# Second attention of a two-layer graph network: row sums from half-added P, and a new place for masks, low halves and statistics

## The reference, cut to what matters

```python
q, k, v = heads(features @ Wq), heads(features @ Wk), heads(features @ Wv)
e = jnp.einsum('whqd,whkd->whqk', q, k)
e = jnp.where(e >= 0, e, ALPHA * e)                      # ALPHA = 0.2
attn = jax.nn.softmax(jnp.where(adj[:, None] > 0, e, NEG), axis=-1)
h = jnp.einsum('whqk,whkd->whqd', attn, v)
out = _layernorm(h, g1, b1)
out = jnp.concatenate([out, features], axis=-1) @ Wffn.T
out = _layernorm(out, g2, b2)
return out + features
```

## Time and profile before

| | us |
|---|---|
| median of 3 runs | 3299.5 (3299.11 to 3303.42) |
| the profiled execution, its own time | 3305.43 |
| its span, first to last instruction | 3303.6 |
| mean granted TensorE clock | 0.98 |
| second attention, about | 1925 to 3303.6 |

### The profile page before, as it was taken

The page is one execution under the profiler, slowest core; times in us unless marked ns, Lnnn a source line. Parts: engine busy times, 40 slices in busy tenths (PEclk is TensorE's granted clock), DMA queues, the critical chain, the costliest instruction groups (busy, mean ns, idle before and its releaser), DMA issues. The chain is left out here.

```text
span 3303.6 us, 77256 instructions
## 1 busy us (share of the span) xinstructions
PE 3136.0 (95%) x29189; PEld 2106.8 (64%) x29189; DVE 2328.4 (70%) x6789; ACT 2009.7 (61%) x3727; POOL 1331.2 (40%) x1254
## 2 busy tenths in 40 slices
PE   7999999999999859999999959999999999999996
PEld 4666666666666536666666636777776677777674
DVE  5888888888888835655555536777777777777773
ACT  3666656666665535665555516676666666666674
POOL 2555555555555523443344321333333333333333
PEclk9999999999999979999999969999999999999998
DMA  5454444444444311111111123444444444444431
GB/s 154 134 145 131 137 140 138 133 137 145 131 135 143 107 58 39 52 50 42 52 52 52 39 83 116 132 134 132 135 134 131 129 130 130 133 138 130 129 124 45
DMA packets 290749, 365.80 MB, mean 111 GB/s; under 512 B 31680, under 2 KB 199232, under 8 KB 290368
## 3 DMA queue, kind: packets, MB, share of 16 engines
q1 hardware_dynamic: 289216, 359.25, 35.6%
q10 hardware_dynamic: 1152, 1.52, 0.2%
HBM read 242.16 MB, written 118.49 MB: 109 GB/s over the span
## 5 line engine op out<-in xcount | busy, mean ns | idle before, releaser
L1840 ACT ACTIVATE b_prob<-b_score_t 128x512 f32<-128x512 f32 x512 | 304.2, 594 | 367.3 <-PE b_score_t L2093 361.3
L2011 DVE CUSTOM_DVE_ANT_0 b_junk<-b_score,b_mask 128x256 bf16<-128x256 f32 x1024 | 390.6, 418 | 190.6 <-issue 183.8
L2428 DVE TENSOR_TENSOR f_gl<-f_act,f_gh 128x512 f16<-128x512 f32 x256 | 245.1, 958 | 285.1 <-ACT f_act L2350 285.1
L1909 POOL TENSOR_TENSOR b_nw_root<-b_nw_var,b_minus_halves 128x2 f32<-128x2 f32 x128 | 89.7, 701 | 841.4 <-DVE b_nw_neg_mean L1961 841.4
L1408 DVE TENSOR_TENSOR a_linked<-a_prob,a_mask 128x1024 f32<-128x1024 f32 x256 | 353.3, 1380 | 3.9 <-ACT a_prob L1205 3.9
L2345 ACT ACTIVATE f_gh<-f_up,s_f_b 128x512 f16<-128x512 f32 x256 | 175.5, 685 | 279.9 <-PE f_up L2476 279.9
L1205 ACT ACTIVATE a_prob<-a_score_t 128x1024 f32<-128x1024 f32 x256 | 259.3, 1013 | 109.6 <-PE a_score_t L1488 102.6
L1401 DVE TENSOR_REDUCE a_neg_max<-a_score 128x4 f32<-128x1024 f32 x256 | 307.0, 1199 | 4.1 <-PE a_score L1501 4.1
L1846 ACT ACTIVATE b_score_t<-b_score_t 128x512 f32<-128x512 f32 x512 | 303.5, 593 | 0.3 <-PE b_score_t L2102 0.3
L2474 PE MATMUL f_down<-s_w,f_gh 128*128 128x256 f16 x1024 | 279.1, 273 | 1.0 <-DVE f_gl L2428 1.0
L2476 PE MATMUL f_down<-s_w,f_gl 128*128 128x256 f16 x1024 | 279.1, 273 | 0.0
(11 more groups left out here) (234 smaller groups left out, 8990.7 us busy)
## 6 DMA issues: line engine op xcount, KB each, us to landing
a_stack<-qk_scratch SPq DMA_DIRECT2D x384, 128.0 KB, 3.0
b_stack<-qk_scratch SPq DMA_DIRECT2D x384, 128.0 KB, 2.8
qk_scratch<-a_qk SPq DMA_DIRECT2D x64, 512.0 KB, 2.9
qk_scratch<-b_qk SPq DMA_DIRECT2D x64, 512.0 KB, 2.8
a_x_sb<-x_t SPq DMA_DIRECT2D x64, 256.0 KB, 3.2
a_adj_sb<-adj_t SPq DMA_DIRECT2D x64, 256.0 KB, 3.2
a_res<-x_nodes SPq DMA_DIRECT2D x64, 256.0 KB, 3.4
after_attention<-a_z_out SPq DMA_DIRECT2D x64, 256.0 KB, 2.5
```

Source lines behind the costliest of these rows:

```text
L1840: nc.scalar.activation(prob[:, he], score_t[s][:].rearrange("p t n -> p (t n)"), ACT.Exp, scale=ALPHA).then_inc(exp_done, 1)
L2011: last = nc.vector.tensor_tensor_reduce(junk[:, s, it], score[s][:, it], mask[:, i, it], -1.0, 3e38, ALU.add, ALU.min, neg_max[:, i, col:c ...
L2428: nc.vector.tensor_tensor(gl[:, bu[1] % 2, f], act32[:, f % 2], gh[:, bu[1] % 2, f], ALU.subtract).then_inc(low_done, 1)
```

## The change

GpSimd gets four additions a graph (`halved`, steps 7, 1, 3 and 5): each adds the two key halves of P for two heads into `half_sum`, 128 x 512 f32. TensorE's sums no longer read P; they are two groups of four products on `half_sum`, `sums0` in step 5 and `sums1` in step 7, behind that step's value products. ScalarE's exp also waits for `half_done` before it overwrites P, and the copy of the sums (`evac_sums`) becomes an operation of its own in step 7. Six entries of `AT` move one step ahead: xh, q_hi, k_hi, v_out, linked and mask. On ScalarE z1, hh and z now stand before the copies of q, k, x and v. On VectorE the low halves stand first in their step and x's ahead of rinv, and statistics of the heads stand ahead of `zero_q`.

```diff
-    AT = {..., "xT": 8, "xh": 9, "xl": 9, "q": 10, "q_hi": 11, "q_lo": 11, "linked": 8, "k": 12, "k_hi": 13, "k_lo": 13,
-          ..., "v": 14, "v_out": 15, ..., "mask": 16, ..., "exp": 29, "values": 33, "res": 45,
-          "evac": 40, "turn_sum": 40, ...}
+    AT = {..., "xT": 8, "xh": 8, "xl": 9, "q": 10, "q_hi": 10, "q_lo": 11, "linked": 7, "k": 12, "k_hi": 12, "k_lo": 13,
+          ..., "v": 14, "v_out": 14, ..., "mask": 15, ..., "exp": 29, "halved": 31, "sums0": 37, "sums1": 39, "values": 33, "res": 45,
+          "evac": 40, "evac_sums": 39, "turn_sum": 40, ...}
+        half_sum = sb("half_sum", [P, H, N], F32)
@@ ScalarE, exp @@
                             act.wait_ge(values_done, n)
+                            act.wait_ge(half_done, n)
@@ ScalarE, copies @@
+                        nc.scalar.activation(heads_sb[:], heads_t[:], ACT.Copy).then_inc(heads_out, 1)
+                    if bv := due(t, h, "evac_sums"):
+                        act.wait_ge(sums_done, count(bv, 2, 2))
+                        if (n := after(back(bv, 1), 1, 1)) is not None:
                             act.wait_ge(sums_turned, n)
-                            act.wait_ge(heads_turned, n)
                         nc.scalar.activation(sums_sb[:], sums_t[:, 0:N], ACT.Copy).then_inc(sums_out, 1)
-                        nc.scalar.activation(heads_sb[:], heads_t[:], ACT.Copy).then_inc(heads_out, 1)
@@ GpSimd @@
+                    if half := half_due(t, h, "halved"):
+                        bv, k = half
+                        pool.wait_ge(exp_done, count(bv, H, 2 * k + 2))
+                        if k % 2 == 0 and (n := after(back(bv, 1), 2, k // 2 + 1)) is not None:
+                            pool.wait_ge(sums_done, n)
+                        pair = prob[:, 2 * k:2 * k + 2]
+                        nc.gpsimd.tensor_tensor(half_sum[:, 2 * k:2 * k + 2], pair[:, :, 0:N], pair[:, :, N:2 * N], ALU.add).then_inc(half_done, 1)
@@ TensorE @@
-                        for term in range(2):
-                            for a in range(HQ):
...
+                        for a in range(HQ):
+                            he = HQ * c + a
+                            last = nc.tensor.matmul(heads_t[DH * a:DH * (a + 1), c], values[...], prob[:, he, cols],
+                                                    start=jt == 0, stop=jt == 1)
+                        last.then_inc(values_done, 1)
+                    for c in range(DC):
+                        if bv := due(t, h, f"sums{c}"):
+                            pe.wait_ge(half_done, count(bv, HALVES, 2 * c + 2))
...
                             for a in range(HQ):
+                                last = nc.tensor.matmul(sums_t[DH * a:DH * (a + 1), 0:N], pick[:, c], half_sum[:, HQ * c + a], start=c == 0, stop=c == 1)
+                            last.then_inc(sums_done, 1)
```

More of the change, by code:

```diff
@@ L1894, in step @@
                         last.then_inc(z_ready, 1)
+                    for j, name in enumerate(("q", "k")):
+                        if bp := due(t, h, name + "_hi"):
+                            i = bp[1] % 2
+                            act.wait_ge(proj_done, count(bp, 4, j + 2))
+                            if j == 0 and exists(back(bp, 2)):
+                                act.wait_ge(qk_stored[i], uses(back(bp, 2), 2) * 16)
+                            nc.scalar.activation(qk[:, i, 2 * j], proj[:], ACT.Copy).then_inc(qk_high, 1)
+                    if bx := due(t, h, "xh"):
+                        act.wait_ge(proj_done, count(bx, 4, 1))
+                        if (n := after(back(bx, XB), 1, 1)) is not None:
+                            act.wait_ge(out_done, n)
+                        nc.scalar.activation(xh[:, bx[1]], proj[:],
+                                             ACT.Copy).then_inc(xh_ready, 1)
+                    if bp := due(t, h, "v_out"):
+                        act.wait_ge(proj_done, count(bp, 4, 4))
+                        if (n := after(back(bp, RING), HALVES, HALVES)) is not None:
+                            act.wait_ge(values_done, n)
+                        nc.scalar.activation(values[:, bp[1] % RING].rearrange("p t n -> p (t n)"), proj[:], ACT.Copy).then_inc(v_ready, 1)
             run_steps(act, step, STEPS_TAIL)
@@ L1975, in step @@
                                                 out_row[:].unsqueeze(1).to_broadcast([P, NT, D]), ALU.add).then_inc(y_ready, 1)
+                    if bx := due(t, h, "xl"):
+                        r = bx[1]
+                        dve.wait_ge(xh_ready, count(bx, 1, 1))
+                        nc.vector.tensor_tensor(xl[:, r], proj[:].rearrange("p (c n) -> p c n", c=DC), xh[:, r], ALU.subtract).then_inc(xl_ready, 1)
                     if bv := due(t, h, "rinv"):
```

60 lines of the change are left out of this document (18 added, 42 removed).

## The result

The changed kernel takes 3218.4 us (median of 4 runs, 3216.0 to 3219.5) where the kernel before takes 3299.3 (4 runs, 3297.7 to 3303.4): a ratio of 0.975, 95% interval 0.9735 to 0.9766, 81 us less. The forecast was 65 us less.

What follows compares the result with a forecast made beforehand. TensorE was taken to bound. Per graph -0.90 - 0.16 - 0.13 + 0.16 = -1.03 us, -59.7 over 58 graphs and -5.4 in six others, so 3299.5 - 65 = 3234.5 us; range 3209 to 3266.

Steps and rivals of the forecast that it cites:

- TensorE bounds, and a group is worth 0.45: TensorE, steps 1 and 3: no room in a graph; two removed groups of sums save 0.90 us a graph.
- The wait of v, -0.16: TensorE ahead of the products of v: the wait for k's low half goes, -0.16 us a graph.
- The DMA stall, -0.13: TensorE before the first score product: an earlier store shortens the DMA wait, -0.13 us a graph, between 0 and -0.18.
- The held-up root, +0.16: GpSimd's root of the heads' statistics, held by zeroing of q, delays TensorE's far product: +0.16 us, bounds 0 and 0.7.
- The slow end of the sum, 3251: Whole kernel: -0.90 + 0.16 = -0.74 us a graph, no wait won back, 48 us less.
- the other six graphs, in ramp and tail, lose their 0.90 each, -5.4: Six graphs outside the 58 whole ones: each loses only the removed groups' 0.90 us, -5.4 us in all.
- Rivals one and three: First: VectorE and the DMA chain bound, 3257 us, chance 0.20; other: late GpSimd queue cancels gain, 3295 to 3303, 0.04.
- rival one: VectorE and the DMA chain bound: graph 19.1 to 19.75 us, chance 0.20; sign, DMA wait over 0.2 us a graph.
- Rival two: GpSimd's queue of six adds delays VectorE's masks and offset pair, so TensorE waits: slower, 3321 us, chance 0.08.
- A late offset pair costs only past +19.2: VectorE's offset pair, held by GpSimd adds: no cost until +19.2 us, when the turn of the maxima wants it.

Runs made afterwards that it cites:

- the first experiment: Kernel before with only the half sums and the two groups of sums on them, old steps and order of ScalarE and VectorE kept: 3336.2 us, ratio 1.011.

## Why the prediction was right, and where it was not

**TensorE bounds, and a group is worth 0.45.** Right. The start distances give 0.43, the run with a group twice 0.43, and the 0.10 us at the change of mode stayed, as the prediction took it. Here the rule of the Trainium skill, "TensorEngine Tiling (Array Packing)", Key Properties (a change of mode drains TensorE), agrees with the trace: the value products alone still take 0.57 to the far product.

**The wait of v, -0.16.** Right: 0.38 became 0.22, with the statistics, k's low half and the store within 0.01 us of where they were worked out. The order alone shows it apart.

**The DMA stall, -0.13.** Somewhat less: the start distance that holds it, from the last transposed scores to the first score product, went from 0.39 on average to 0.31, -0.08; the order alone brought 0.09.

**The held-up root, +0.16.** That zeroing holds the root was right, the price was not. The root is held by 0.37 us, not 0.6, and TensorE shows no wait for it: the turn of z and the far product start 0.44 apart, as they did. The sum has no term for the 0.07 of waiting for the relu in step 5, which comes from z's place on ScalarE. The terms as measured, -0.86, -0.16, -0.08 and +0.07, give -1.03 again, which is luck: the misses cancel. Measured is -1.09; the last 0.06 are spread over distances that each differ by a hundredth or two. In the 58 graphs it is -63.3 us for -59.7. The slow end of the sum, 3251, has 0.16 for the root again, and not the 0.7 that was named as its bound; nothing came of it.

**The step that failed: "the other six graphs, in ramp and tail, lose their 0.90 each, -5.4".** With what lies around them they lost 22.6 in the two profiled executions and some 18 by the medians (1.7 of it ahead of the stage, which the change cannot have done). This term was mis-sized, and it is most of why 81 us were measured and not 65. I priced start and tail as if TensorE bounded them too. In the start it is not TensorE's work that counts, but the order: with VectorE's old order start and first three graphs are back at 43.4 and 62.5 us; with the new order (reciprocal first) and the old sums they are at 36.5 and 54.5. The places of the masks count too, 39.5 us of start with them in step 0. What of it falls to which link of the chain product, copy, low half, product was not measured. I had costed VectorE's order only by the one wait it removed in a full graph.

**What the sum did not say.** It read -0.90 as the yield of the sums and -0.29 as that of the order, as if they were separate. Taken in that sequence they nearly are: the order (reciprocal first) gives -0.24, and the half sums on top of it another -0.85. Taken the other way they are not: the sums alone give +0.60. TensorE's removed time was the time in which x's, q's and k's low halves became ready; without the new order it comes back as waits, 1.24 us of them in the run with VectorE's old order. And the adds, which cost nothing in the new places, cost 0.47 us a graph at the turn of the maxima in the old ones, as the distances of the first experiment say. Even the order alone depends on what it stands beside: with the reciprocal behind x's low half, as the changed kernel has it, it gives +0.09 on the old sums, and does no harm on the new ones, which start in step 5. The forecast came near because it laid the whole new order behind its inputs.

**Rivals one and three.** Neither came. The DMA stall is 0.09 us a graph by the start distances (3.7 / 58 = 0.06 in the list), under the 0.2 that was named as the sign of rival one; the store goes at +9.79 and not at +10.5; and TensorE's list has no wait for a half sum.

**Rival two.** Its place was right but its threshold was not: "A late offset pair costs only past +19.2". Between the pair and the turn of the maxima stands y, 0.69 us long, and the turn waits for it too. In the changed kernel the pair ends at +18.4 and y about 0.1 us before it would cost; the masks in step 0 or a longer queue of adds use that up at once. There were thus 0.1 us of cover where the prediction counted 0.8. That GpSimd holds VectorE up and costs nothing in the changed order is now measured (no adds: 19.12).

## What to carry to other kernels

When work leaves the bounding engine, list what was becoming ready on the others during that time: it can be late by as much unless their order changes too, and an experiment with half of such a change can show the opposite sign. Read start-to-start distances beside the list of waits, and compare the number of products with that of weight loads, before a wait of the same small size in every round is believed. Price the filling of a pipeline by its own chain, not by the share of the bounding engine.

## What was unexpected of the hardware

Some of VectorE's instructions that lie wholly in SBUF were held by a GpSimd instruction beside them: a mask of 0.42 us took 1.49, the other 1.04, `neg_some` of 0.18 took 0.72 at most, and GpSimd's root of 0.69 took 1.08 beside the zeroing. The statistics of the heads, in SBUF too, were not held beside a half sum (0.407 to 0.428 us), nor were those with an input in PSUM (y 0.69, low halves 0.68, maxima 0.407 to 0.424). So "wholly in SBUF" is not the test; which instruction it is counts. The Trainium skill, "SBUF — State Buffer", Who interferes with whom, has this as an exclusive lock on a pair of ports that only some instructions of VectorE use. The trace agrees, with the held and the untouched rows above.

The lock was expected; that it could take 123 us of an engine without moving the end was not. With the copies late, a gap of 3 us in each graph was followed by twelve products of TensorE at the 1.2 GHz level, 2.53 us for 1.31, so the gap cost some 40% more than itself. I had expected nothing of the clock in this change.
